# Two inverse square roots in a transformer layer on one core: from VectorE's own iteration to a power on GpSimd

## What is computed

```python
out = einsum('bhqk,bhkv->bhqv', softmax(s1) - lam * softmax(s2), v)   # causal, values 32 wide
normed = (out - mean(out)) * rsqrt(var(out) + 1e-5)                   # per token and head
x = layernorm(x + merged(normed * (1 - LAM_INIT)) @ Wo)               # per token, over 256
x = layernorm(x + ffn(x))
```

## Time and profile before

| what | us |
|---|---|
| median of 3 runs | 1914.19 (1912.91 to 1914.51) |
| the profiled execution | 1914.51 |
| its span, first to last instruction | 1910.7 |
| attention, first exponential corner to the last finish_tile | 166.1 to 1181.9 |
| the last head: copy of its first tile's sums to its end | 1116.7 to 1181.9 |
| first matmul of the finish phase | 1185.2 |

### The profile page before, as it was taken

One profiled execution on the slowest core, in us unless ns is written; L12 is line 12 of the kernel. 1 busy time (PEld: TensorE's weight loads), 2 busy tenths in 40 slices (PEclk: granted clock), 3 DMA queues, 4 the chain that ended last, 5 costly groups with the idle time before them and its releaser, 6 DMA issues. The chain is left out here.

```text
span 1910.7 us, 30778 instructions
## 1 busy us (share of the span) xinstructions
PE 1855.0 (97%) x12160; PEld 1062.8 (56%) x12160; DVE 1031.3 (54%) x1999; ACT 1408.5 (74%) x1701; POOL 232.3 (12%) x308
## 2 busy tenths in 40 slices
PE   7997999999999999999999998999999999999996
PEld 6773333333333333333333334888888888888885
DVE  5554664566556555566556654445545454636342
ACT  4446999999999999999999995544445454545452
POOL 3001111111121112211211120000000000000000
PEclk9998999999999999999999999999999999999998
DMA  8877076435643565346633621001000101000000
GB/s 275 256 244 162 10 116 122 74 66 111 116 83 71 98 116 90 74 87 116 113 63 75 117 60 45 4 30 34 12 34 12 34 12 34 12 34 22 1 11 13
DMA packets 130143, 146.08 MB, mean 76 GB/s; under 512 B 74228, under 2 KB 100468, under 8 KB 122356
## 3 DMA queue, kind: packets, MB, share of 16 engines
q1 hardware_dynamic: 129272, 142.46, 34.2%
q10 hardware_dynamic: 720, 1.57, 0.2%
HBM read 101.79 MB, written 39.06 MB: 74 GB/s over the span
## 5 line engine op out<-in xcount | busy, mean ns | idle before, releaser
L897 ACT ACTIVATE attn_probs<-attn_s_ps 128x1024 f32<-128x1024 f32 x1088 | 1002.7, 1121 | 20.4 <-PE attn_s_ps L923 19.9
L946 PE MATMUL attn_sums_ps<-attn_probs,heads_v 128*32 128x512 f32 (+3 forms) x5120 | 587.5, 540 | 0.0
L923 PE MATMUL attn_s_ps<-heads_q,heads_k 50*128 50x512 f32 (+3 forms) x2560 | 450.9, 427 | 12.8 <-DVE heads_q L1026 12.4
L923 PEld LDWEIGHTS attn_s_ps<-heads_q,heads_k 50*128 50x128 f32 x2560 | 212.9, 185 | 448.1 <-ACT attn_probs L897 401.8
L1614 ACT ACTIVATE split_whole<-split_hid_ps,scales 128x512 f32<-128x512 f32 x128 | 88.3, 690 | 274.1 <-PE split_hid_ps L1528 273.9
L878 POOL TENSOR_SCALAR_AFFINE_SELECT attn_probs<-attn_probs 128x512 f32<-128x512 f32 x256 | 180.1, 715 | 841.9 <-ACT attn_probs L897 841.9
L1528 PE MATMUL split_hid_ps<-split_hid_b,ffn_r 128*128 128x512 f32 x1024 | 240.8, 392 | 0.0
L1528 PE MATMUL split_hid_ps<-split_hid_a,ffn_r 128*128 128x512 f32 x1024 | 238.0, 391 | 0.0
L1528 PEld LDWEIGHTS split_hid_ps<-split_hid_a,ffn_r 128*128 128x128 f32 x1024 | 190.1, 188 | 41.0 <-DVE split_hid_a L1753 1.0
L1528 PEld LDWEIGHTS split_hid_ps<-split_hid_b,ffn_r 128*128 128x128 f32 x1024 | 189.8, 188 | 38.2
L946 PEld LDWEIGHTS attn_sums_ps<-attn_probs,heads_v 128*32 128x32 f32 x5120 | 107.6, 108 | 174.5 <-issue 140.0
(11 more groups left out here) (165 smaller groups left out, 1665.4 us busy)
## 6 DMA issues: line engine op xcount, KB each, us to landing
heads_q_raw<-qk_raw SPq DMA_DIRECT2D x60, 384.0 KB
heads_k_raw<-qk_raw SPq DMA_DIRECT2D x60, 384.0 KB
qk_raw<-proj_copies SPq DMA_DIRECT2D x64, 256.0 KB, 2.4
values<-proj_v SPq DMA_DIRECT2D x8, 1024.0 KB, 5.8
diffs<-attn_diff SPq DMA_DIRECT2D x32, 256.0 KB, 4.1
heads_k_raw<-ones SPq DMA_DIRECT2D x60, 128.0 KB
heads_v<-values SPq DMA_DIRECT2D x15, 512.0 KB, 19.1
heads_spare<-in_ffn SPq DMA_DIRECT2D x30, 256.0 KB, 9.6
```

Of the source, the lines that this page charges most:

```text
L897: nc.scalar.activation(weights, side_by_side, ACT.Exp, scale=SCALE).then_inc(exp_done, 1)
L923: last = nc.tensor.matmul(s_ps[(NU * h + n) % SLOTS][:, s, col:col + width], k_sb[u][rows, b * SEQ + j * PARTS:b * SEQ + (j + 1) * PARTS], ...
L946: last = nc.tensor.matmul(sums[c * D:(c + 1) * D, off:TILE], v_sb[u][:, b * KEY_BLOCKS + j, :], probs[k % PROBS][:, b, s, place:place + wi ...
```

## The change

The power function on POOL takes the place of `inverse_root`. At the start of attention POOL sets a column `half` to 0.5. In the last head, after the corners of step 9 (VAR_AT), POOL waits for `head_var` and raises it to the power 0.5 (TENSOR_TENSOR with `pow`, 128x64); after the corners of step 31 (MID_AT = END[2] + 11) it does the same with the 128x4 `var`. DVE waits for the root, refines it once (reciprocal, product, sum) and takes the reciprocal: four instructions in place of eleven, and five in place of twelve for the second root. The scale factor in L1152 changes with it.

```diff
+        half = room.sb("half", [PARTS, 1])
+        VAR_AT = END[1]
+        MID_AT = END[2] + 11
         def _(pool):
+            pool.memset(half[:, :], 0.5).then_inc(half_set, 1)
             for h in range(HEADS):
                 for k in range(NS):
                     if not CORNERS[k]:
                         continue
...
+                    if h == LAST and k == VAR_AT:
+                        pool.wait_ge(half_set, 1)
+                        pool.wait_ge(early_var_ready, 1)
+                        pool.tensor_tensor(early["head_root"][:, :], head_var[:, :], half[:, :].to_broadcast([PARTS, SUBS * HEADS]), ALU.pow).then_inc(early_root_ready, 1)
                     if h == LAST and k == WIDE_AT:
                         pool.wait_ge(wide_ready, 1)
                         pool.partition_all_reduce(keep["wide_col"][:, 1:2], keep["wide_col"][:, 0:1], PARTS, bass.bass_isa.ReduceOp.max).then_inc(wide_reduced, 1)
+                    if h == LAST and k == MID_AT:
+                        pool.wait_ge(early_mid_var_ready, 1)
+                        pool.tensor_tensor(early["norm"]["root"][:, :], early["norm"]["var"][:, :], half[:, :].to_broadcast([PARTS, SUBS]), ALU.pow).then_inc(early_mid_root_ready, 1)
...
             def early_rstd():
-                dve.wait_ge(early_var_ready, 1)
-                inverse_root(head_var, early["head_root"], early["head_quotient"], early["head_rstd"], early_vec, 0)
+                root, quotient = early["head_root"], early["head_quotient"]
+                dve.wait_ge(early_root_ready, 1)
+                nc.vector.reciprocal(quotient[:, :], root[:, :]).then_inc(early_vec, 1)
+                dve.wait_ge(early_vec, 1)
+                nc.vector.tensor_tensor(quotient[:, :], quotient[:, :], head_var[:, :], ALU.mult).then_inc(early_vec, 1)
+                dve.wait_ge(early_vec, 2)
+                nc.vector.tensor_tensor(quotient[:, :], quotient[:, :], root[:, :], ALU.add).then_inc(early_vec, 1)
+                dve.wait_ge(early_vec, 3)
+                nc.vector.reciprocal(early["head_rstd"][:, :], quotient[:, :]).then_inc(early_vec, 1)
+                dve.wait_ge(early_vec, 4)
...
             def early_mid_norm():
-                dve.wait_ge(early_mid_var_ready, 1)
-                inverse_root(bufs["var"], bufs["root"], bufs["quotient"], bufs["quotient"], early_mid_vec, v0)
-                nc.vector.tensor_scalar(bufs["rstd"][:, :], bufs["quotient"][:, :], 2.0 ** ROOT_STEPS, None, ALU.mult).then_inc(early_mid_vec, 1)
-                dve.wait_ge(early_mid_vec, v0 + 3 * ROOT_STEPS + 3)
+                dve.wait_ge(early_mid_root_ready, 1)
+                nc.vector.reciprocal(quotient[:, :], root[:, :]).then_inc(early_mid_vec, 1)
+                dve.wait_ge(early_mid_vec, v0 + 1)
+                nc.vector.tensor_tensor(quotient[:, :], quotient[:, :], bufs["var"][:, :], ALU.mult).then_inc(early_mid_vec, 1)
+                dve.wait_ge(early_mid_vec, v0 + 2)
+                nc.vector.tensor_tensor(quotient[:, :], quotient[:, :], root[:, :], ALU.add).then_inc(early_mid_vec, 1)
+                dve.wait_ge(early_mid_vec, v0 + 3)
+                nc.vector.tensor_scalar(quotient[:, :], quotient[:, :], 0.5, None, ALU.mult).then_inc(early_mid_vec, 1)
+                dve.wait_ge(early_mid_vec, v0 + 4)
+                nc.vector.reciprocal(bufs["rstd"][:, :], quotient[:, :]).then_inc(early_mid_vec, 1)
+                dve.wait_ge(early_mid_vec, v0 + 5)
```

More of the change, by code:

```diff
@@ L695 @@
 EARLY_COLUMNS = 8448
-ROOT_BITS = float(0x1fbd1df5)
-ROOT_STEPS = 3
 def early_buffers(nc):
@@ L729, in attention_sems @@
              "shift_ready", "shift_added", "cut_high", "cut_done", "w_loaded", "w_rounded", "compared", "wide_ready", "wide_reduced",
-             "head_squared", "head_summed", "x_in", "wo_in", "heads_in", "heads_whole", "early_wo_high", "early_wo_low", "early_var_ready",
+             "head_squared", "head_summed", "x_in", "wo_in", "heads_in", "heads_whole", "early_wo_high", "early_wo_low", "early_var_ready", "early_root_ready",
              "early_vec", "early_normed", "early_turned", "early_high", "early_low", "early_projected", "early_added", "early_mid_vec", "early_mid_var_ready",
-             "early_mid_ready")}
+             "early_mid_root_ready", "early_mid_ready", "half_set")}
     sems["values_loaded"] = [room.sem(f"attn_values_loaded{u}") for u in range(2)]
@@ L805, in attention_phase @@
              "stacks_loaded", "values_loaded"))
[L806 to L809, removed]
+        (head_squared, head_summed, x_in, wo_in, heads_in, heads_whole, early_wo_high, early_wo_low, early_var_ready, early_root_ready, early_vec, early_normed,
+         early_turned, early_high, early_low, early_projected, early_added, early_mid_vec, early_mid_var_ready, early_mid_root_ready, early_mid_ready, half_set) = (sems[name] for name in (
+             "head_squared", "head_summed", "x_in", "wo_in", "heads_in", "heads_whole", "early_wo_high", "early_wo_low", "early_var_ready", "early_root_ready", "early_vec", "early_normed",
+             "early_turned", "early_high", "early_low", "early_projected", "early_added", "early_mid_vec", "early_mid_var_ready", "early_mid_root_ready", "early_mid_ready", "half_set"))
         STORES = 16 * BATCH
         KNOWN = LAST * D
+        VAR_AT = END[1]
         WIDE_AT = END[1] + 2
+        MID_AT = END[2] + 11
         EARLY = {END[1] + 4: [("turn", 0)], END[1] + 7: [("project", 0)], END[1] + 8: [("turn", 1)], END[1] + 10: [("project", 1)],
@@ L1125, in early_wo @@
                 nc.vector.tensor_tensor(early["wo"][1][:, :, :], early["wo_raw"][:, :, :], early["wo"][0][:, :, :].bitcast(F32), ALU.subtract).then_inc(early_wo_low, 1)
[L1127 to L1139, removed]
-            def early_rstd():
-                dve.wait_ge(early_var_ready, 1)
-                inverse_root(head_var, early["head_root"], early["head_quotient"], early["head_rstd"], early_vec, 0)
+            def early_rstd():
+                root, quotient = early["head_root"], early["head_quotient"]
[8 more added lines that the diff above has]
+                dve.wait_ge(early_vec, 4)
                 dve.wait_ge(heads_in, 16)
@@ L1151, in early_norm @@
                 rstd = early["head_rstd"][:, s * HEADS:(s + 1) * HEADS].unsqueeze(2).to_broadcast([PARTS, HEADS, D])
-                nc.vector.scalar_tensor_tensor(rows, rows, 2.0 ** ROOT_STEPS * (1.0 - LAM_INIT), rstd, ALU.mult, ALU.mult).then_inc(early_normed, 1)
+                nc.vector.scalar_tensor_tensor(rows, rows, 2.0 * (1.0 - LAM_INIT), rstd, ALU.mult, ALU.mult).then_inc(early_normed, 1)
             def early_split(n, high, low):
@@ L1187, in early_mid_norm @@
                 bufs = early["norm"]
+                quotient, root = bufs["quotient"], bufs["root"]
                 v0 = 2 * SUBS
-                dve.wait_ge(early_mid_var_ready, 1)
-                inverse_root(bufs["var"], bufs["root"], bufs["quotient"], bufs["quotient"], early_mid_vec, v0)
-                nc.vector.tensor_scalar(bufs["rstd"][:, :], bufs["quotient"][:, :], 2.0 ** ROOT_STEPS, None, ALU.mult).then_inc(early_mid_vec, 1)
-                dve.wait_ge(early_mid_vec, v0 + 3 * ROOT_STEPS + 3)
+                dve.wait_ge(early_mid_root_ready, 1)
[9 more added lines that the diff above has]
+                dve.wait_ge(early_mid_vec, v0 + 5)
                 for s in range(SUBS):
```

## The result

The changed kernel takes 1937.3 us (median of 4 runs, 1936.12 to 1939.83), the one before 1913.84 beside it: 23.5 us more, ratio 1.0122 with a 95% interval of 1.011 to 1.0135. The forecast was 7.8 us more; its side was right, and the time lies 5.3 us above the range. The profiled execution after took 1934.14 us, its span 1932.4 against 1910.7.

The account below looks back on a forecast made before the run. PE, full from about 1128 us in the last head, was taken as the bound; stalls of 4.77 and 3.07 us sum to 7.8, added to the median 1914.2 for 1922.0 us, range 1916 to 1932.

Parts of the forecast that it names:

- What bounds: Last head: PE is full from about 1128 on, so whatever stops PE moves the end; freeing only DVE does not.
- What goes: DVE's saved root work: worth nothing at the first root, at most 0.14 us of PE wait at the second.
- Three changes of sets: POOL in the last head: power, all-reduce, power need three code changes, each a pair of 6.13 us.
- The power: On POOL, taken as twenty multiplications: 2.6 us for 128x64 (bracket 0.13 to 12 us), 0.26 us for 128x4.
- first stall: After step 9's corners, pair and power delay the corner of step 11, making PE's weigh(11) 4.77 us late.
- Second stall: After step 31's corners, pair, power and five DVE instructions make PE's turn_mid(0) 3.07 us late.
- Clock: Rival, 12%: PE's clock drops after a stall, some 3.4 us lost each; 1925.4, or 1928.8 if both do.
- dear power: Rival, 13%: the 128x64 power takes above 6 us, first stall 8 us and more; 1931.9 at the bound.
- Middle: Second pair, ahead of the all-reduce, 1133.2 to 1139.3: hidden, since step 17's corners are due at 1141.2.
- DVE behind the first root: DVE takes the sums by 1136.3, before turn_heads(0) is due at 1137.85, so no more delay is added.
- the rest follows as above: Under a slow first power, DVE's root is as late as the corner, and what follows goes as in the forecast.

Follow-up runs that it names:

- set_early_mult: Changed kernel without the second all-reduce, with a tiny POOL multiplication at the start of attention and multiplications for both powers: 1914.66 us, ratio 1.0004.
- mult: Changed kernel with both powers made multiplications, so the roots and output are other numbers: 1925.2 us, ratio 1.0056.
- after_full: Changed kernel with PE's two waits filled with 108 and 32 repeated score matmuls: 1932.91 us, ratio 1.0102.
- after_corner: Changed kernel with the first pair and power behind the corner of step 11 in place of ahead of it: 1938.72 us, ratio 1.0129.
- set_early_busy: Changed kernel without the second all-reduce, with an early tiny POOL multiplication and 28 repeated score matmuls in PE's wait before weigh(11): 1924.97 us, ratio 1.0053.

## Why the prediction was wrong, step by step
**What bounds.** Right: only waits of PE from weigh(11) on counted, and each of them counted in full. 14.2 + 5.3 us of wait are in the end of the span.
**What goes.** Right: at most 0.14 us; `set_early_mult` shows the DVE time saved is worth nothing measurable.
**Three changes of sets.** Right in number and place. Each pair was taken at 6.13 us, from a place where the all-reduce's set came in; measured are 7.53 and 7.03 ahead of the powers (6.7 to 7.5 in the last heads of the nine kernels that have such a pair) and 5.98 ahead of the all-reduce (5.8 to 6.2). So 6.13, an upper bound for the one direction, was none for the other, and a pair costs about 1 us more in the direction that matters, 2.3 us in the sum. The Trainium skill (GPSIMD Engine Reference, section 2.1, Instruction dispatch) gives 5.95 us for the first call to freshly loaded code. That agrees with the gap ahead of the all-reduce and is low for the other set. Of the 1 to 2 us allowed for busy DMAs little can be there: in the six kernels with both, the second pair ahead of a power, in a stretch without DMAs, is 0.05 to 0.7 us shorter than the first. No run separates that cause from others.
**The power, the step that failed.** "A power is a chain of multiplications; I take twenty of them, 2.6 us" was a guess in the lower part of a bracket of 0.13 to 12 us, and it measures 10.57 (what it is made of, no run shows), 0.158 us a column, close to the all-reduce's 0.187 that bounded it. With the measured sizes the prediction's own sums give 1123.80 + 7.53 + 10.57 + 0.64 + 0.1 - 1128.46 = 14.2 us for the first stall, the time measured. It was 8.0 of the missing 15.7 us. The second power, 1.05 for 0.26, adds 0.8. The range, unlike the forecast, allowed for this: the power alone would have given about 1931.
**Second stall.** 3.07 reckoned, 5.34 measured (5.48 less the 0.14 of before): 0.9 from the pair, 0.8 from the power, and 0.6 from DVE's five instructions, 1.62 us where 1.05 was reckoned (last section).
**Clock, the term that the sum put at nothing.** Kept as a rival with 12%, at 3.4 us a stall, and apart from the dear power with 13%. Both came. The prediction treated them as one or the other, though its own stall of 4.8 us was enough to bring the clock down: `mult` stood for 3.48 us and had weigh(11) at 1.08 us behind it. Measured are 2.1 and 1.5 us, 3.6 by the stretches, 4.3 to 4.9 by `after_full` (its two stalls are 0.5 us shorter as well). This is where the range failed: it ended at 1932 because its upper end was the power's bound with no clock added. 1931.9 + 3.6 would have reached 1935.5, and with the pairs' 2.3 about the time measured.
**Middle, and DVE behind the first root.** Right: the pair before the all-reduce is hidden, and no wait is shown at turn_heads(0). But "the rest follows as above" hid a second wait of the same length, which `after_corner` shows.
What stays open is why the two directions of a change of sets cost 6 and 7 us, and why the lower clock lasts 5 us after one wait and 9 after another.

## What to carry to other kernels
An engine that is idle 88% of the time can still be in the way: what is put into its queue stands ahead of its next small task, so reckon from the moment that task is due, and look for a second consumer of the same result before moving it. An operation that no row shows needs a measurement, not a guess inside a wide bracket; here a trial in an idle gap of the same engine would have given it. Reckon a stall of PE with its clock, in the forecast and at the end of the range: behind the stalls here, of 3.5 to 25 us, the work ran at the lower level for some microseconds more.

## What the runs showed of the hardware
A power on GpSimd costs 0.158 us a column of 128 partitions and 0.44 fixed, 36 times the multiplication over 64 columns (10.52 against 0.29 us), for any base or exponent tried. Going between the all-reduce and TENSOR_TENSOR takes 5.8 to 6.2 us one way and 6.7 to 8.1 the other (the 8.1 in `set_early_busy`, at the start of attention), which no record of its own shows: only a pair MODIFY_POOL_CONFIG of some ns ahead of a gap.
Small DVE operations with two inputs are stretched beside POOL's corners. DVE's timeline after the change, while two corners run from 1190.80 to 1192.03:
```profile
1190.84 0.18 DVE L1196 RECIPROCAL early_mid_quotient<-early_mid_root 128x4 f32<-128x4 f32 x1 [6.28 <-POOL early_mid_root L894]
1191.05 0.40 DVE L1198 TENSOR_TENSOR early_mid_quotient<-early_mid_quotient,early_mid_var 128x4 f32<-128x4 f32 x1
1191.48 0.56 DVE L1200 TENSOR_TENSOR early_mid_quotient<-early_mid_quotient,early_mid_root 128x4 f32<-128x4 f32 x1
1192.08 0.17 DVE L1202 TENSOR_SCALAR early_mid_quotient<-early_mid_quotient 128x4 f32<-128x4 f32 x1
1192.28 0.18 DVE L1204 RECIPROCAL early_mid_rstd<-early_mid_quotient 128x4 f32<-128x4 f32 x1
```
Both operations with two inputs take 0.40 and 0.56 us where 0.16 is usual, and end about when a corner does (1191.45 and 1192.04, the corners at about 1191.4 and 1192.03). The reciprocal at 1190.84, with one input and beside the same corners, takes its 0.18. `mult` shows the same, 0.37 and 0.56 us. The Trainium skill (GPSIMD Engine Reference, section 8, Key points) says that the two engines share their SBUF interfaces and contend where DVE has two SBUF inputs; these rows agree.
